# Row sums of squares on VectorE, whole-tile hand-offs and the loading order in a transformer layer kernel

## What is computed

```python
x = x + 0.5 * ffn(layernorm(x))          # ffn: h @ sign(weight).T, 1024 x 1024
x = x + attn(layernorm(x))               # linear attention, 16 heads of 64
x = x + 0.5 * ffn(layernorm(x))

# attn: Q = phi(h Wq.T + bq), K = phi(h Wk.T + bk), V = h Wv.T + bv, phi = elu + 1
# KV = sum over the sequence of K V^T, Z = sum of K
# out = (Q KV) / (Q Z + 1e-6), then out @ Wo.T + bo
```

## Time and profile before

| what | us |
|---|---|
| time, median of 2 runs | 2113.0 (2071.1 and 2154.9) |
| profiled execution, time | 2072.0 |
| profiled execution, span of the slowest core (core 0) | 2070.5 |
| spans of the eight cores | 2061.7 to 2070.5 |
| mean granted clock of TensorE, by core | 0.989 to 0.993 |
| busy: PE, ACT, DVE, POOL | 1737.9, 1233.4, 799.4, 148.0 |

### The profile page before, as it was taken

How to read it: one execution, slowest core, us unless ns; L and a number is a source line. 1 busy time by engine, 2 the same in 40 slices (tenths; PEclk the granted TensorE clock), 3 DMA queues, 4 the chain that set the end, 5 groups by cost and what they waited for, 6 DMA issues and landing times.

```text
span 2070.5 us, 33315 instructions; the slowest of 8 cores (2061.7 to 2070.5 us)
## 1 busy us (share of the span) xinstructions
PE 1737.9 (84%) x10592; PEld 792.0 (38%) x10784; DVE 799.4 (39%) x2241; ACT 1233.4 (60%) x2025; POOL 148.0 (7%) x274
## 2 busy tenths in 40 slices
PE   0588898898898888988889889778888888888887
PEld 0233333333333333333333333344444444444443
DVE  2233343343433333433334333144444444444443
ACT  1466767767667767676776776644444444444443
POOL 1000000000000001000000000011101001101100
PEclk9999999999999999999999999989999999999999
DMA  8622222222222223222222222123333233333331
GB/s 183 124 90 67 89 90 66 89 80 77 89 69 88 90 67 120 90 65 89 67 89 88 69 89 61 57 103 117 113 128 125 105 128 123 114 122 128 117 113 77
DMA packets 134634, 199.37 MB, mean 96 GB/s; under 512 B 88384, under 2 KB 88384, under 8 KB 134464
## 3 DMA queue, kind: packets, MB, share of 16 engines
q0 software_dynamic: 32960, 109.08, 15.6%
q1 hardware_dynamic: 101504, 88.15, 14.1%
HBM read 104.87 MB, written 83.89 MB: 91 GB/s over the span
## 4 chain that ended last, share of the span: by engine, by line
PE 52%; ACT 25%; issue 15%; DVE 4%; DMA 3%; ACTq 1%; DVEq 0%; SPq 0%
PE pA L471 22%; PE pA L482 12%; PE pA L602 11%; ACT u1b L450 4%; ACT mnb L405 3%; ACT mxb L407 3%; DVE y2t L346 2%; PE pA L604 2%; PE pA L486 2%; ACT nb L365 2%; ACT kbQ L393 2%; ACT eb L406 2%; PE pA L476 2%; ACT attnfm L437 2%; DMA stg<-wfT 2%
## 5 line engine op out<-in xcount | busy, mean ns | idle before, releaser
L482 PE MATMUL pA<-wv,u1fm 128*128 128x512 bf16 x961 | 231.8, 383 | 110.3 <-ACT kbK L409 110.2
L602 PE MATMUL pA<-wo,attnfm 128*128 128x512 bf16 x960 | 233.9, 386 | 36.1 <-ACT attnfm L439 34.9
L482 PE MATMUL pA<-wk,u1fm 128*128 128x512 bf16 x1023 | 242.3, 379 | 18.4 <-ACT kbQ L393 18.3
L450 ACT ACTIVATE u1b<-y2t 128x1024 bf16<-128x1024 f32 x64 | 67.6, 1056 | 291.4 <-DVE y2t L346 291.4
L471 PE MATMUL pA<-sw,u0fm 128*128 128x512 bf16 x1023 | 236.2, 384 | 0.2 <-issue 0.2
L482 PE MATMUL pA<-sw,u2fm 128*128 128x512 bf16 x1023 | 233.3, 381 | 1.7 <-ACT u2fm L445 1.5
L471 PE MATMUL pA<-wq,u1fm 128*128 128x512 bf16 x962 | 218.1, 379 | 9.9 <-issue 9.9
L482 PEld LDWEIGHTS pA<-wv,u1fm 128*128 128x128 bf16 x1024 | 90.8, 98 | 213.4 <-issue 123.8
L390 ACT ACTIVATE u2b<-y1t 128x1024 bf16<-128x1024 f32 x63 | 66.6, 1057 | 176.4 <-DVE y1t L288 176.4
L288 DVE SCALAR_TENSOR_TENSOR y1t<-pA,xt 128x1024 f32<-128x1024 f32 x63 | 77.1, 1224 | 197.2 <-PE pA L471 197.2
L602 PEld LDWEIGHTS pA<-wo,attnfm 128*128 128x128 bf16 x1024 | 91.5, 98 | 140.3 <-issue 52.1
(11 more groups left out here) (123 smaller groups left out, 2504.8 us busy)
## 6 DMA issues: line engine op xcount, KB each, us to landing
xt<-x SPq DMA_DIRECT2D x64, 512.0 KB, 3.9
y1scr<-y1t POOLq DMA_DIRECT2D x64, 512.0 KB, 3.8
y1in<-y1scr POOLq DMA_DIRECT2D x64, 512.0 KB, 3.8
out<-y3t SPq DMA_DIRECT2D x64, 512.0 KB, 2.6
qscr<-qfm POOLq DMA_DIRECT2D x64, 256.0 KB, 3.1
qfin<-qscr POOLq DMA_DIRECT2D x64, 256.0 KB, 3.9
qfm<-phiQ SPq DMA_TRANSPOSE x512, 2.3
stg<-wfT SPq DMA_DIRECT2D x4, 512.0 KB, 9.2
```

What stands on the lines that cost most here:

```text
L450: e.activation(u1b[:, 0, :], y2t[:, tw % 2, :], AF.Square, accum_out=sq3b[:, :]).then_inc(sSq3, 1)
L482: mm = e.matmul(dst[:, h*512:(h+1)*512], lhs_fm[:, c*P:(c+1)*P], w_sb[:, c, h*512:(h+1)*512], start=(c == 0), stop=(last and c == 7))
L602: e.matmul(pA2[:, h*512:(h+1)*512], attnfm[:, (t - 1) % 2, c*P:(c+1)*P], wo[:, c, h*512:(h+1)*512], start=(c == 0), stop=False)
```

## The change

- **Loading order (SP):** the four x tiles are issued first, then the eight chunks.
- **Pass 1:** ACT's Squares of y1t (L381, L390) go. The DVE squares y1t itself, directly behind the instruction that makes it, with a self-wait on either side. The statistics of y1t (tile t+1) are no longer worked out before the sums of x (tile t+3), but after them, in one merged call for both.
- **Pass 2:** ACT's Square of y2t (L450) goes, and the DVE squares y2t. y2t is one instruction over 1024 columns behind the whole of Wo instead of two over 512; red3a and the addition of the two sums go. Wo is a call of `proj` with chunks outside and halves inside, which starts on attnfm's first half and signals once at the end. FFN2 also has chunks outside; it waits for the whole of y2t at its start, and for the halves of u2fm.

```diff
-            stg_chunk(0)
-            stg_chunk(1)
             for t0 in range(4):
                 s, j = t0 // NJ, t0 % NJ
                 e.dma_start(out=xt[:, t0 % 4, :], in_=x[s, j*P:(j+1)*P, :]).then_inc(dIn[t0 % 4], 16)
-            for c in range(2, 8):
-                stg_chunk(c)
+            for c in range(8):
+                ...
@@ POOL
-                e.wait_ge(vY2, 2 * (t - 1))
+                e.wait_ge(vY2, t - 1)
@@ DVE, pass 1
                     v.scalar_tensor_tensor(y1t[:, (t + 1) % 2, :], pA1[:, :], 0.5, xt[:, (t + 1) % 4, :],
                                            ALU.mult, ALU.add, accum_out=red2b[:, :]).then_inc(vY1, 1)
-                if t + 1 < NT:
-                    v.wait_ge(sSq2, t + 2)
-                    if t >= 2:
-                        v.wait_ge(sR02, t)
-                    ln_stats_multi(v, vsync, [(red2b, sq2b, vr2, (t + 1) % 2, negm2, mS2)]
-                                   )[0].then_inc(vVr2, 1)
+                    v.wait_ge(vY1, t + 2)
+                    vsync(v, v.scalar_tensor_tensor(u2b[:, 0, :], y1t[:, (t + 1) % 2, :], 0.0,
+                                           y1t[:, (t + 1) % 2, :],
+                                           ALU.bypass, ALU.mult, accum_out=sq2b[:, :]))
                 if t + 3 < NT:
                     tf = t + 3
                     v.wait_ge(dIn[tf % 4], 16 * (tf // 4 + 1))
                     v.reduce_sum(red1b[:, :], xt[:, tf % 4, :], axis=AX.X)
                     vsync(v, v.scalar_tensor_tensor(y2t[:, 0, :], xt[:, tf % 4, :], 0.0, xt[:, tf % 4, :],
                                            ALU.bypass, ALU.mult, accum_out=sq1b[:, :]))
+                specs = []
+                if t + 1 < NT:
+                    if t >= 2:
+                        v.wait_ge(sR02, t)
+                    specs.append((red2b, sq2b, vr2, (t + 1) % 2, negm2, mS2))
+                if t + 3 < NT:
                     if t >= 1:
                         v.wait_ge(sR01, t)
-                    ln_stats_multi(v, vsync, [(red1b, sq1b, vr1, (t + 3) % 4, negm1, mS1)]
-                                   )[0].then_inc(vVr1, 1)
+                    specs.append((red1b, sq1b, vr1, (t + 3) % 4, negm1, mS1))
+                if specs:
+                    outs = ln_stats_multi(v, vsync, specs)
+                    if t + 1 < NT:
+                        outs[0].then_inc(vVr2, 1)
+                    if t + 3 < NT:
+                        outs[-1].then_inc(vVr1, 1)
@@ DVE, pass 2
-                    v.wait_ge(tWo, 2 * t - 1)
+                    v.wait_ge(tWo, t)
-                    v.scalar_tensor_tensor(y2t[:, tw % 2, 0:512], pA2[:, 0:512], 0.0,
-                                           y1in[:, tw % 2, 0:512],
-                                           ALU.bypass, ALU.add, accum_out=red3a[:, :]).then_inc(vY2, 1)
-                    v.wait_ge(tWo, 2 * t)
-                    v.scalar_tensor_tensor(y2t[:, tw % 2, 512:1024], pA2[:, 512:1024], 0.0,
-                                           y1in[:, tw % 2, 512:1024],
+                    v.scalar_tensor_tensor(y2t[:, tw % 2, :], pA2[:, :], 0.0, y1in[:, tw % 2, :],
                                            ALU.bypass, ALU.add, accum_out=red3b[:, :]).then_inc(vY2, 1)
-                    v.wait_ge(vY2, 2 * t)
-                    vsync(v, v.tensor_tensor(red3b[:, :], red3a[:, :], red3b[:, :], ALU.add))
-                    v.wait_ge(sSq3, t)
+                    v.wait_ge(vY2, t)
+                    vsync(v, v.scalar_tensor_tensor(u1b[:, 0, :], y2t[:, tw % 2, :], 0.0,
+                                           y2t[:, tw % 2, :],
+                                           ALU.bypass, ALU.mult, accum_out=sq3b[:, :]))
@@ ACT
-                if t + 1 < NT:
-                    e.wait_ge(vY1, t + 2)
-                    e.activation(u2b[:, 0, :], y1t[:, (t + 1) % 2, :], AF.Square,
-                                 accum_out=sq2b[:, :]).then_inc(sSq2, 1)
...
-                    e.wait_ge(vY2, 2 * t)
-                    e.activation(u1b[:, 0, :], y2t[:, tw % 2, :], AF.Square,
-                                 accum_out=sq3b[:, :]).then_inc(sSq3, 1)
@@ PE, pass 2
-                    e.wait_ge(sU2fm, 2 * t - 4)
+                    e.wait_ge(vY2, min(t - 1, NT))
...
-                         hw=(vY2, min(2 * t - 3, 2 * NT - 1)))
+                         cw=(sU2fm, 2 * t - 5))
...
-                    e.wait_ge(sAttnfm, 2 * t)
                     if t >= 3:
                         e.wait_ge(vY3, t - 2)
-                    for h in range(2):
-                        for c in range(8):
-                            e.matmul(...)
-                        e.matmul(...)
+                    proj(e, attnfm[:, (t - 1) % 2, :], wo, pA2[:, :], bor, tWo,
+                         cw=(sAttnfm, 2 * t - 1))
```

More of the change, by code:

```diff
@@ L97, in build_nc @@
         sq2b = sb("sq2b", [P, 1], F32)
-        red3a = sb("red3a", [P, 1], F32)
         red3b = sb("red3b", [P, 1], F32)
@@ L159, in _ @@
         def _(e):
-            def stg_chunk(c):
+            for t0 in range(4):
+                s, j = t0 // NJ, t0 % NJ
+                e.dma_start(out=xt[:, t0 % 4, :], in_=x[s, j*P:(j+1)*P, :]).then_inc(dIn[t0 % 4], 16)
+            for c in range(8):
                 buf = stg[:, 0, :] if c % 2 == 0 else y3t[:, 0, :]
@@ L166, in stg_chunk @@
                 e.dma_start(out=buf, in_=wfT[c*P:(c+1)*P, :]).then_inc(gStg, 16)
-            stg_chunk(0)
-            stg_chunk(1)
-            for t0 in range(4):
-                s, j = t0 // NJ, t0 % NJ
-                e.dma_start(out=xt[:, t0 % 4, :], in_=x[s, j*P:(j+1)*P, :]).then_inc(dIn[t0 % 4], 16)
-            for c in range(2, 8):
-                stg_chunk(c)
             for t in range(NT):
@@ L275, in _ @@
                                    ALU.mult, ALU.add, accum_out=red2b[:, :]).then_inc(vY1, 1)
-            v.wait_ge(sSq2, 1)
+            v.wait_ge(vY1, 1)
+            vsync(v, v.scalar_tensor_tensor(u2b[:, 0, :], y1t[:, 0, :], 0.0, y1t[:, 0, :],
+                                   ALU.bypass, ALU.mult, accum_out=sq2b[:, :]))
             ln_stats_multi(v, vsync, [(red2b, sq2b, vr2, 0, negm2, mS2)])[0].then_inc(vVr2, 1)
@@ L379, in _ @@
                              scale=r01[:, :], bias=nb1[:, :]).then_inc(sU0, 1)
-            e.wait_ge(vY1, 1)
-            e.activation(u2b[:, 0, :], y1t[:, 0, :], AF.Square,
-                         accum_out=sq2b[:, :]).then_inc(sSq2, 1)
             e.wait_ge(vVr2, 1)
@@ L596, in _ @@
                 if 1 <= t <= NT:
-                    e.wait_ge(sAttnfm, 2 * t)
                     if t >= 3:
                         e.wait_ge(vY3, t - 2)
-                    for h in range(2):
-                        for c in range(8):
-                            e.matmul(pA2[:, h*512:(h+1)*512], attnfm[:, (t - 1) % 2, c*P:(c+1)*P],
-                                     wo[:, c, h*512:(h+1)*512], start=(c == 0), stop=False)
-                        e.matmul(pA2[:, h*512:(h+1)*512], ones_row[0:1, :],
-                                 bor[0:1, h*512:(h+1)*512], start=False,
-                                 stop=True).then_inc(tWo, 1)
+                    proj(e, attnfm[:, (t - 1) % 2, :], wo, pA2[:, :], bor, tWo,
+                         cw=(sAttnfm, 2 * t - 1))
                 if t < NT:
```

1 line of the change is left out of this document (removed).

## The result

The changed kernel is slower: 2215.1 us (median) against 2072.8 us, a ratio of 1.068 with a 95% interval of 1.066 to 1.071. The profiled execution took 2213.2 us, its slowest core (core 3) 2211.6 us. The forecast was 2190 us, its range 2120 to 2235. So the sign and the main causes held, and 23 us were missing from the sum.

A forecast was written before the change was run, and what follows sets the result against it. Pass 1 was taken as bound by a ring of PE and ACT, pass 2 by a ring through y2t, its statistics, attnfm and Wo. The sum was 2072 + 59 + 50 + 10 - 1 = 2190 us, range 2120 to 2235.

The forecast's parts named there:

- Part 1: Pass 1: y1t's statistics reach ACT 0.96 us late in 61 tiles, 59 us in all (42 to 79).
- their cover: Pass 1: u1b would release the U1 transposes at 526.86, while the PE is busy with K's matmuls until about 527.
- The price of the square: DVE square with two f32 SBUF operands: taken from L300 as 1.22 us, against 2.4 by the skill's half-rate rule.
- rival 5: Both passes: a DVE square takes twice the 1.22 us, 151 us more than the forecast, 2341 us; chance 0.02.
- rival 3: Pass 1: the late statistics are hidden, DVE pieces starting about 0.9 us apiece, 2081 or 2066 us; chance 0.05.
- Part 2: Pass 1: PE clock falls in the longer gap before V, 30 tiles at 1.65 us, 50 us (0 to 100).
- The nearest row: Pass 1: two tiles with a 1.79 us gap on eight cores; applying their share of falls gives 69 us.
- Rival 1: Pass 1: the PE's clock holds in the longer gap before V, 2140 us; chance 0.24.
- rival 2: Pass 1: the clock falls at nearly every tile, 55 of 61, 2231 us; chance 0.12.
- Part 3: Loading: with x first, wfT's later chunks land later and the last Sign comes 10 us later (7 to 13).
- Part 4: Pass 2: three branches meet at Wo, y2t's spacing 10.95 against 10.97 us, -1 us in all (-13 to +25).
- Rival 4: Pass 2: FFN2 behind the full read of y2t becomes last branch, +0.4 a tile, 2165 or 2215 us; chance 0.10.

The follow-up runs named there:

- e4_fill: The changed kernel with ten extra 512-column matmuls, results never read, filling the PE's wait before V in pass 1: 2143.2 us, 1.025 against the kernel before.
- e3: The kernel before with y1t's square on the DVE, its statistics still worked out directly behind it, ahead of x's sums: ratio 1.002.
- e5: The kernel before with ACT's Square of y1t kept, but y1t's statistics behind the sums of x and merged with x's: ratio 1.000.
- e12: The changed kernel with ACT's copies of K moved ahead of Q's third activation: 2124.7 us, 1.0225 against the kernel before.
- e9: The kernel before with the change's pass 2 part, the DVE's wait for Wo put behind its two satisfied waits: 0.9989 against the kernel before.
- e10: The kernel before with ACT's copies of K moved ahead of Q's third activation: 2009.6 us, 0.970.

## Why the prediction was right, and where it was off

**Part 1 (late statistics): right, term by term.** Forecast from the start of y1t: square 1.40, reduction 2.80, x's square 3.93, statistics 5.33, vr 6.25, ACT 6.50, late by 0.96. Measured: 1.34, 2.75, 3.88, 5.35, 6.25, 6.50, late by 0.96 (20.58 - 19.62). The forecast 59 us over 61 tiles are 59.1 in e4_fill as a mean and 61 on core 3, where the kernel before has no falls. That the 0.96 agrees to the hundredth is luck: single terms are off by up to 0.06, and the 0.27 for the four extra small instructions was a choice between 0 and 0.60. The U1 transposes kept their cover: in the tile shown the PE goes from K into them at 554.84 without an idle time. e3 and e5 add what the forecast didn't say: either half of this edit is free by itself.

**The price of the square: right.** It takes 1.23 us with two f32 operands in SBUF (both are the same tile; two different ones weren't measured), no more than y1t with one operand in PSUM. The rule of the Trainium skill (Vector Engine (DVE) Microarchitecture Reference, Points that are easy to get wrong), that such an instruction runs at half the rate, isn't borne out by any run here; rival 5 falls. So does rival 3, since the 1024-wide pieces start 1.13 to 1.41 us apart, as worked out.

**Part 2 (clock): the mechanism right, the size too small.** This is the term that was mis-sized. It held 30 falls of 1.65 us, 50 us. It measured 47 falls of 1.59 on core 3, 75 us, and 69.3 us in the mean of all cores when e4_fill is taken off (1348.7 - 1279.4); e4_fill's own pass 1 is 4 us longer than 61 x 20.58 + 19.6, which accounts for most of the difference. The fall's price was right within 4%; the count was not. The nearest row of the trace had 11 of 16, which gives 42 falls and 69 us, nearly what was measured; I had halved it on the argument that sixteen cases are few. Few cases widen a range, but they are no reason to move the value away from them, and here the new gap (2.47 us) was even longer than the one of the sample (1.79). That the 69 us come out so near is partly luck all the same: the cores mostly fall in the same tiles, so the sixteen cases were hardly more than the two moments they came from, and e12 shows 25 falls in 61 at a wait not much shorter than theirs. Rival 1 (the clock holds, 2140) falls with the window's 0.94; rival 2 (55 falls, 2231) was too many.

**Part 3 (loading): the mechanism right, the size too high and inside its bounds by luck.** Forecast +10 with bounds 7 and 13 (the upper one is 12 by its own terms: 25.6 + 47 - 60.3); the last Sign is 7.6 us later in the mean. c0 landed at 12.8 (forecast 12.5) and c1 at 16.6 (16.2). The weights were issued at 18.7, not 17, and c2 landed at 20.25, near the quick end of 19.9. From there to the last Sign it was 44.2 us where the sum had five chunks of 9.4, 47. So both terms were too high, and on core 0, whose rows the sum used, the delay was only 4.1 us, under the low bound. The mean is higher because core 0's last Sign had been the latest of the eight before (60.3 against a mean of 57.0).

**Part 4 (pass 2): wrong by 11 us, inside its own bound of 25.** The chain was forecast as vr 3.45, ln 3.70, y3t 5.17, U2 transposes 6.23, Wo 6.7, y2t 10.95. Measured 3.39, 3.64, 5.27, 6.17, 6.75, 11.14. Up to Wo nothing is off by more than 0.1. The step that failed is the last one, "y2t starts 0.17 later": from Wo to y2t it is 4.39 us where the sum had 4.26. e9 shows why: the DVE has two satisfied waits behind the one for Wo, 0.14 us together, which the sum put at nothing, and with the order turned round Wo to y2t is 1623.65 - 1619.39 = 4.26 us and the tile 11.01. The rest, 0.05, is Wo's own start; whether y3t or the U2 transposes release it, which differ by less than 0.1 us, wasn't told apart. Rival 4 had FFN2's wait for the whole y2t as the cause: it ends at +1.48 instead of 1.38, 0.1 of its 0.4, and so isn't the main one.

**The sum.** 2072 + 59 + 69 + 8 + 10 = 2218, against 2213.2 measured in the profiled execution. The forecast had 59 + 50 + 10 - 1; the clock (+19) and pass 2 (+11) are what it lacked, and loading (-2) is what it had too much. The other 5 us are in what the stage table leaves out: from the last y2t to the end it is 18.0 us in before and 15.7 in after (means), and the slowest core lies 5.6 us above the mean span in before and 3.2 in after.

**What remains open: which tiles the clock falls in.** With a wait before V of 0.32 (e4) and 0.57 us (e10) it fell on no core. With 2.48 us it fell in 47 of 61. With about 1.5 us it fell in none but the two disturbed tiles in the profile of the kernel before, in 17 and 14 tiles on two cores in e3, and in 25 of 61 in e12, with the same wait and the same work in front of it. The length of this one wait therefore isn't all that counts, and no run here tells what else does. It isn't chance core by core either: in e12 all eight cores agree in 44 of the 62 tiles, and every second tile falls for long stretches.
